# Four graph layers on one core: source tiles cut at multiples of 128 blocks, their addresses computed from one word

## What is computed

```python
x = _layernorm(x + L0(x, edge_attr))        # mean of edge_attr by src, three matmuls with ReLU and batch norm
x = _layernorm(x + L1(x))                   # relu((mean over edges of x[src], by dst, + x) @ W.T + b)
x = _layernorm(x + L2(x, edge_type))        # messages by type, mean by dst, a matmul, layer norm, GELU
x = _layernorm(x + L3(x, edge_weight))      # see below

def _L3_gnn_ref(node_features, edge_index, edge_weight, W, b, gamma, beta):
    ...
    norm = dinv[row] * w * dinv[col]
    x = node_features @ W
    msg = x[row] * norm[:, None]
    out = jax.ops.segment_sum(msg, col, num_segments=N) + b
    ...
```

## Time and profile before

| | us |
|---|---|
| median of three runs | 3749.47 (3747.87 to 3751.64) |
| the profiled execution | 3743.15 |
| its span | 3741.4 |
| mean granted clock of PE | 0.964 |

### The profile page before, as it was taken

One profiled execution on the slowest core, in us unless ns is written; L12 is line 12 of the kernel. 1 busy time (PEld: TensorE's weight loads), 2 busy tenths in 40 slices (PEclk: granted clock), 3 DMA queues, 4 the chain that ended last, 5 costly groups with the idle time before them and its releaser, 6 DMA issues.

```text
span 3741.4 us, 94994 instructions
## 1 busy us (share of the span) xinstructions
PE 2820.6 (75%) x23282; PEld 2453.3 (66%) x23283; DVE 2495.4 (67%) x7099; ACT 1517.8 (41%) x4312; POOL 1847.8 (49%) x2243
## 2 busy tenths in 40 slices
PE   8555544444439986887799689999999958887996
PEld 6232322222229975777799479999899957776995
DVE  7666666666647778555577777777666777554667
ACT  0111100000004445555577543222365348886765
POOL 4777777777763341777433354444521007774000
PEclk9999999999999997999899899999999989998998
DMA  6444444444448943778698035555378807885883
GB/s 216 150 150 141 149 143 146 147 143 149 141 131 285 292 144 104 279 274 280 216 293 274 9 115 175 177 179 183 126 241 248 263 30 273 272 283 194 289 286 123
DMA packets 419041, 721.75 MB, mean 193 GB/s; under 512 B 68624, under 2 KB 198169, under 8 KB 417932
## 3 DMA queue, kind: packets, MB, share of 16 engines
q1 hardware_dynamic: 330492, 494.35, 42.7%
q0 software_dynamic: 88464, 226.43, 16.1%
HBM read 481.26 MB, written 285.09 MB: 205 GB/s over the span
## 4 chain that ended last, share of the span: by engine, by line
PE 42%; POOL 23%; issue 13%; DMA 11%; DVE 5%; ACT 3%; SPq 2%; DVEq 2%; POOLq 1%; ACTq 0%
PE ps L1375 20%; POOL slots L750 19%; PE ps L1408 9%; DMA gbuf<-ring_raw,to_blk 8%; PE ps L1410 5%; POOL gbuf L804 3%; DMA ring_raw<-gbuf 2%; PE ps L1420 2%; PE ps L1250 2%; PE ps L1461 1%; DVEq L501 1%; PE ps L1452 1%; DVE stats L1935 1%; SPq L501 1%; ACT ring_raw L976 1%
## 5 line engine op out<-in xcount | busy, mean ns | idle before, releaser
L804 POOL DMA_INDIRECT gbuf<-ring_raw,to_blk x774 | 754.4, 975 | 727.4 <-DVE ring_raw L1868 257.9
L750 POOL DMA_INDIRECT slots<-ring_raw,idx_edges x782 | 751.4, 961 | 242.2 <-issue 242.2
L1375 PE MATMUL ps<-ring_raw,memory 128*128 128x128 f32 (+2 forms) x6576 | 784.6, 279 | 82.6 <-DVE memory L1836 49.2
L1375 PEld LDWEIGHTS ps<-ring_raw,memory 128*128 128x128 f32 x6576 | 764.5, 193 | 104.9 <-issue 56.3
L1836 DVE TENSOR_TENSOR memory<-dst_lane,lane_ids 128x512 f32<-128x512 f32 x774 | 535.1, 692 | 74.8 <-POOL dst_lane L768 51.7
L1286 PE MATMUL ps<-memory 128*49 128x343 bf16 (+6 forms) x784 | 263.5, 489 | 387.9 <-DVE memory L1732 386.6
L1408 PE MATMUL ps<-memory 128*128 x2752 | 497.8, 273 | 9.9 <-DVE memory L1877 7.5
L1846 DVE TENSOR_TENSOR memory<-memory,ps 128x128 f32 (+2 forms) x1032 | 294.6, 285 | 308.3 <-PE ps L1375 294.8
L935 ACT ACTIVATE memory<-lane_ids,dst_lane 128x128 f32<-128x128 f32 x1032 | 330.3, 392 | 403.2 <-PE ps L1375 246.1
L1410 PE MATMUL ps<-memory 128*128 x2752 | 477.4, 220 | 0.0
L1286 PEld LDWEIGHTS ps<-memory 128*49 128x49 bf16 x784 | 113.9, 159 | 530.4 <-DVE memory L1732 301.6
(11 more groups left out here) (283 smaller groups left out, 4781.6 us busy)
## 6 DMA issues: line engine op xcount, KB each, us to landing
ring_raw<-gbuf SPq DMA_DIRECT2D x669, 268.0 KB, 3.6
ring_raw<-in_edge_attr SPq DMA_DIRECT2D x111, 448.0 KB, 3.8
ring_raw<-slots SPq DMA_DIRECT2D x153, 272.0 KB, 4.1
zr<-lane_rows SPq DMA_DIRECT2D x87, 384.0 KB
zt<-lane_rows SPq DMA_DIRECT2D x87, 384.0 KB
memory<-lane_rows SPq DMA_DIRECT2D x84, 384.0 KB, 4.8
memory<-slots SPq DMA_DIRECT2D x105, 272.0 KB, 4.1
memory<-gbuf SPq DMA_DIRECT2D x105, 268.0 KB, 3.8
```

The source lines that it names most:

```text
L750: pool.indirect_dma_start(edges, bass.IndirectOffsetOnAxis(idx_edges[0:n, u, j:j + 1], 0), edge_rows[0:n, u, j, :], None).then_inc(scatter ...
L804: pool.indirect_dma_start(gbuf, bass.IndirectOffsetOnAxis(to_blk[:, t:t + 1], 0), node_rows[:, r, :], None, bounds_check=NBLK - 1, oob_is_ ...
L1375: ins = pe.matmul(bank(r % 3, width), hots[:, r, j * P:(j + 1) * P], rows[:, j, 0:width], start=j == 0, stop=j == BLK - 1)
```

## The change

The source tiles of the gathers are cut elsewhere. Blocks of the sorted list are taken 128 at a time from the list's start, whatever group they belong to: SPANS = 210 spans, 35 rounds (SR) of six. Where a group ends within a span, two groups share it. A pair of group and span is a step, and there are at most 210 + 49 - 1 = 258 of them, the same number as tiles before.

- `gather(1)` and `gather(3)`: PE still takes 258 steps, but a step adds to its span's bank, so a span with two groups gets two steps of matmuls and is copied and sent once. Four banks are used in turn. Ahead of its four matmuls a step does a matmul of one column with zeros (`new_bank`), which opens the next span's bank. ACT and POOL take 210 spans. `gather(2)` and its 258 sends are as before, over the new steps.
- PE takes one 16-bit word a round from `step_words`. It says which of the six steps begin a new span; from it PE computes for each step the bank, the next bank, the nodes' column and the count of `staged` to wait for. ACT takes three such words a round from `span_words`, for the counts of `gathered` it waits for.
- `reduce(0)` goes over the same 258 steps. Its payload now has nine words (`P_TYPED`, lane and type in one), and ACT keeps it by span, at a place it loads from a table (`at_pay`), and the target block of each step apart (`to_of`).
- DVE makes the new tables after the old ones (`span_tables`). POOL has two more operations on the payload at the start and fewer between `reduce(0)` and `gather(1)`.

```diff
+SPANS = -(-MAXB // P)
+SR = SPANS // RING
+BANKS = 4
...
-    return RR * (layer - 1)
+    return (0, SR, SR + RR, SR + RR + SR)[layer - 1]
...
-PAY = 8
-P_ONE, P_TYPE, P_W, P_DST, P_SRC, P_TO = 0, 1, 4, 5, 6, 7
+PAY = 9
+LIST = PAY - 1
+P_ONE, P_TYPE, P_W, P_DST, P_SRC, P_TYPED, P_TO = 0, 1, 4, 5, 6, 7, 8
...
+            steps.link(pool.tensor_scalar(pay8[:, :, P_TYPED], type_i, float(P), -float(P), ALU.mult, ALU.add))
+            pool.wait_ge(pays_ready, 7)
+            pool.tensor_tensor(pay8[:, :, P_TYPED], pay8[:, :, P_TYPED], pay8[:, :, P_SRC], ALU.add).then_inc(pays_ready, 1)
...
+                to = to_blk if layer == 2 else to_span
...
-                for i in range(RR):
+                for i in range(RR if layer == 2 else SR):
                     for r in range(RING):
                         scatter_block(i, r)
...
-            def keep_pays(h, odd):
+            def keep_pays(h, odd, at):
                 i = h * 2 + odd
                 for r in range(RING):
                     rows = rows_of(0, r, odd).rearrange("p (k w) -> p k w", k=BLK)
                     wait_rows(act, 0, h, r, odd)
-                    act.copy(pays[:, bass.ds(i * RING + r, 1), :].rearrange("p a (k w) -> p (a k) w", k=BLK),
+                    act.copy(to_of[:, bass.ds(i * RING + r, 1)], rows[:, 0, D + P_TO:D + P_TO + 1])
+                    act.wait_ge(pays_kept, i * RING + (RING + r))
+                    act.copy(pays_raw[:, bass.ds(at[r], BLK * PAY)].rearrange("p (k w) -> p k w", k=BLK),
                              rows[:, :, D:ROW_A]).then_inc(pays_kept, 1)
...
+                def send_round(i):
+                    words = nc.values_load_multi_w_load_instructions(
+                        span_words[:, bass.ds(i * (RING // 2), RING // 2)], engines=[ACT_E], min_val=0, max_val=65535,
+                        skip_runtime_bounds_check_because="words of 16 bits")[1]
                     for r in range(RING):
                         at = i * RING + r
-                        act.wait_ge(gathered, i * RING + (RING + base + r + 1))
+                        if r % 2 == 0:
+                            count = (words[r // 2] & 511) + (RING + GATHERED[layer])
+                        else:
+                            count = count + (words[r // 2] >> 9)
+                        act.wait_ge(gathered, count)
...
-                def gather_tiles(i):
-                    at = loaded(at_x, None, i, PE, (GROUPS - 1) * D)
+                def new_bank(to):
+                    pe.matmul(ps_flat[:, to], ident_h[:, :], none_h, start=True, stop=True, skip_group_check=True)
...
+                def gather_steps(i):
+                    word = nc.values_load_multi_w_load_instructions(
+                        step_words[:, bass.ds(i, 1)], engines=[PE], min_val=0, max_val=D * SPANS - 1,
+                        skip_runtime_bounds_check_because="the table holds such words")[1][0]
+                    first = (word >> 7) + STAGED[layer]
+                    span = word & 0x7F80
                     for r in range(RING):
+                        if r:
+                            span = span + (word & (2 << r)) * (D >> (r + 1))
+                        to = in_bounds((span * 4) & (BANKS - 1) * 512, (BANKS - 1) * 512)
+                        upon = in_bounds((span * 4 + 512) & (BANKS - 1) * 512, (BANKS - 1) * 512)
+                        node = in_bounds(i * (RING * D) + r * D - span, (GROUPS - 1) * D)
+                        if r == 3:
+                            first = first + (word & 3)
+                        pe.wait_ge(staged, first + (r % 3 + RING + 2 - BANKS))
+                        new_bank(bass.ds(upon, 1))
                         pe.wait_ge(src_hots, i * RING + (base + r + 1))
-                        pe.wait_ge(staged, i * RING + (base + r + 1))
                         for j in range(BLK):
-                            ins = pe.matmul(bank(r)[:, j * P:(j + 1) * P], hots[:, r, j * P:(j + 1) * P],
-                                            nodes[:, bass.ds(at[r], D)], start=True, stop=True)
+                            ins = pe.matmul(ps_flat[:, bass.ds(to + j * D, D)], hots[:, r, j * P:(j + 1) * P],
+                                            nodes[:, bass.ds(node, D)], start=False, stop=j == BLK - 1,
+                                            skip_group_check=True)
                         ins.then_inc(gathered, 1)
```

## The result

The kernel before ran in 3750.55 us (median of 4 runs, 3747.87 to 3754.14), the changed one in 3929.98 us (median of 4, 3928.31 to 3933.58): a ratio of 1.0486, 95% interval 1.0472 to 1.0500. The change makes this kernel 4.9% slower. Forecast were 3910 us and a range of 3825 to 4000.

What follows compares the result with a forecast made beforehand. POOL's sends, 1.28 us each, were taken to bound the gathers, and PE's sequencer after the change. 3743.15 us + 156 (gathers) + 5 (elsewhere) = 3904, with 6.3 for the median of runs 3910; range 3825 to 4000.

Steps and rivals of the forecast that it cites:

- POOL bounds before, PE's sequencer after: Gathers 1 and 3: POOL's sends at 1.28 us bound now; after the change PE's register instructions, about 0.10 us each, do.
- The round: Six steps of PE in gathers 1 and 3: 7.9 us of steps, 0.6 head, 1.2 load, together 9.7 us.
- The step: PE in gathers 1 and 3: 12 register instructions at 0.10 us plus five matmuls at 0.02, 1.30 us.
- The load: PE's register load each round of gathers 1 and 3, one word in place of six: taken as 1.2 us.
- The tail: POOL's work behind the last matmul of gathers 1 and 3 shrinks to the last send, giving back 9 us a stage.
- `gather(1)` +81: Layer 1 gather: 417 us of rounds, less 327.1 now and 9 of tail, makes it 81 us longer.
- `gather(3)` +75: Layer 3 gather: 417 us of rounds, less 333.5 now and 9 of tail, makes it 75 us longer.
- Elsewhere +5: `reduce(0)` +3 us for ACT's added copies and load, `span_tables` +2 us on DVE, POOL's added passes nothing.
- ACT and four banks "no cost": Gathers 1 and 3: a bank is asked for again 8 us later, ACT needs one to two: no cost.
- Rival 1: Gathers 1 and 3: register work hides behind queued matmuls, the array bounds, 288 us a stage, 3652 us total; chance 0.13.
- Rival 3: Gathers 1 and 3: array at the lower 1.2 GHz clock throughout, 533 us a stage, 4143 us total; chance 0.04.
- Queued matmuls behind a control instruction: PE: the skill's queuing rule would support hiding; the prediction held that rows 5 contradict it for matmuls with register-computed addresses.

Runs made afterwards that it cites:

- the loads of one word: Kernel before, with one 32-bit word loaded a round in place of six, used for all six tiles: 3752.22 us in one run.
- the smallest dose: Kernel before, each matmul's PSUM address computed in registers to the same value, 6 sequencer instructions a step (3 before) in five of six steps: 3750.13 us, ratio 1.0006.
- the doses: Kernel before, PSUM addresses computed in registers to unchanged values, with 6, 10 or 12 sequencer instructions in five of six steps: 3750.13, 3807.4 and 3905.0 us.
- the kernel with 16-bit tables: Changed kernel with bank, next bank, node and span loaded from a table, 24 words of 16 bits a round, instead of computed: 4390.34 us, ratio 1.1714.
- the fastest table kernel: Changed kernel with six banks, tables of 20 32-bit words, one wait for three steps, two rounds a loop turn: 3701.95 us, ratio 0.9875 to the kernel before.

## Why the prediction was right, point by point

**POOL bounds before, PE's sequencer after: right.** That POOL bounds before is shown by the loads of one word and by the smallest dose, which both leave the stages as they were. That the register work alone is enough for the loss is shown by the doses, and that it is the cause in the changed kernel itself by what less of it gives: 0.24 us a step for two instructions less, and 3702 us with all of the change but the arithmetic, the four banks and some waits, which were not taken away one by one from the changed kernel.

**The round: 9.7 us forecast, 9.76 measured, by two errors that cancel.** That is the mean from load to load in `gather(1)` (409.8 us for 42 rounds, by the row of loads below); 43 times the sum counts one head more than the stage has between its first and last matmul. The step was 1.48 us, not 1.30. Five of its instructions were mis-sized. Two of them, which compute the next bank and the node's address in four operations each, take 0.17 us from start to start where I had 0.10 for all: the price of a register instruction was taken from a few short ones. Three that stand ahead of a matmul take 0.13, not 0.12. Together 2 x 0.07 + 3 x 0.01 = 0.17. The sequencer's rows of the step from 1700.84 on (min/median/max ns, first and last start) show the long ones by the largest durations, 112 and 113 ns where the earlier trace rows had at most 46:

```profile
L1477 PEldq FUSED_REGOPS  x2: 42/77/112, 1701.1 to 1701.3; - x2
```

```profile
L1500 PEldq FUSED_REGOPS  x5: 42/51/113, 1701.5 to 1702.2; - x5
```

The load was the other error: 0.29 us in the median of `gather(1)` and 0.32 of `gather(3)`, where I had taken 1.2 between 0.89 and 1.75.

```profile
L1483 PEldq TENSOR_LOAD <-at_blk x43: 285/288/549, 1474.3 to 1884.1; - x43
```

```profile
L1483 PEldq TENSOR_LOAD <-at_blk x43: 283/317/545, 3172.1 to 3593.2; - x43
```

I had bounded a load of one word by loads of six and twelve, and scaled only by the DMA share. So 6 x 1.48 + 0.54 of head + 0.29 = 9.71. Against the forecast the steps are 1.0 us a round too small and the load 0.9 too large: that the sum fits is luck, and a range made from 0.09 to 0.107 us an instruction did not hold the 0.17 of a long one. The upper end of the range was also added up wrong: 0.107 and 1.75 give a round of 10.8 us and about 4010 in all, not 10.9 and 4022. The branch took its 0.2 us as before (208 ns, 207 in the earlier trace rows).

**The tail: right.** 9.3 and 8.9 us given back, 9 forecast.

**`gather(1)` +81 forecast, +81.8 measured; `gather(3)` +75 forecast, +87.5 measured.** The missing 12.5 us are layer 3's. Its instruction for the node's address has one operation more and lasts 131 ns instead of 113 (the row below), which adds 0.02 us to each step. Its fourth step has one more register instruction, 0.1. The load is 0.05 longer in the mean. That is 0.12 + 0.1 + 0.05 = 0.27 a round, x 43 = 11.6 us. The prediction used one round for both layers without looking at layer 3's own instructions.

```profile
L1500 PEldq FUSED_REGOPS  x1: 131/131/131, 3302.1 to 3302.1; - x1
```

**Elsewhere +5 forecast, +8.1 up to the end of `reduce(0)`.** ACT's copies did go in pairs 0.33 us apart (0.4 forecast). In the changed kernel and seven of its kin the start of `reduce(0)` lies at 1112.8 to 1115.8 us and the stage lasts 256.1 to 259.9, against 1110.0 to 1111.2 and 251.1 to 252.7 in the kernel before and four of its kin: 4 and 6 us in the mean, so this part was too small by half, for both together. The other 8.2 us of the table lie in stretches that the change doesn't touch. Half of them is the dense stage behind `reduce(1)`, 118.9 us before and 122.8 after; the dose of 6, with the code of before in that stage, has 121.3, and those of 10 and 12 have 122.6. So I take it as scatter between executions; the one of before that was profiled was a short one, 7 us under its median.

**ACT and four banks "no cost": right at this pace only.** In `gather(1)` of the changed kernel the instruction that waits for a bank starts 0.10 us behind the one before it in the mean of each step but the first, and 0.15 there, so there is next to no such wait. With less register work the four banks, with ACT's computed bank beside them, cost 61 us in one kernel and 189 in another.

**Rival 1 (the register work hides)** is out for this change, and its deciding point was put rightly where the sequencer passes the other bounds. Its time for full hiding, 3652, is 50 us under the 3702 of the kernel that comes closest. Of these `gather(1)` has 8 (296 us from first to last matmul against 288, a step being 1.00 us and not 0.95) and `gather(3)` 31 (319 us, with its waits for banks and longer gaps behind the loads); the rest is the smaller tail and the time elsewhere. **Rival 3 (the lower clock all through)** is out: the granted clock in the gathers was 0.99 and 0.98. It did show up where I hadn't looked for it, behind PE's 6 us stops in the kernel with 16-bit tables.

**Queued matmuls behind a control instruction.** Matmuls that were already queued did go on while a control instruction ran: in the timeline of the kernel with 16-bit tables, weight loads start until 1608.90 + 0.97 us, 1.5 us into a load of registers that began at 1608.4. To that extent the trace agrees with the Trainium skill's "Advanced Engine Details and Errata", Sequencer Loop. But only about twelve weight loads were queued at that point, and a matmul whose address was still to be computed was not among them: in the changed kernel the array stands idle 0.43 to 0.45 us in each of the steps shown above.

## What to carry to other kernels

Count the instructions of an engine's sequencer per step as a resource of its own, with the number of operations in each, and compare that sum with the array's time and with the slowest partner's: below the largest of them register work is free, above it each instruction counts in full, 0.1 to 0.17 us here. A change that takes work off the bounding engine by giving another one arithmetic should put the arithmetic into a table made once, and load it in 32 bits. When one bound is lifted, look again at the buffers that were ample before: four PSUM banks cost nothing at 2.0 us a span, and, with 0.2 us more of ACT's own between its wait and its copy, 61 and 189 us in kernels that could have run at 1.8 and 1.6.

## What the runs showed of the hardware that I had not expected

**Loads into registers.** The loads of 16-bit words went by the piece: one 0.29 us, three on ACT 0.90 in the median (0.30 each), 24 on PE 7.4 (0.31 each). Those of 32-bit words did not: in `gather(1)` one took 0.41 in the median, six 1.6 to 1.7, 20 took 1.8 and 24 took 2.2. Twelve in layer 2 took 0.9, so that the place counts more than the number. The DMA share was 0.77 in the one and 0.50 in the other, but it alone doesn't explain it: ACT's twelve in `reduce(0)` of the changed kernel took 0.78, at a share of 0.89. It stays open.

**Fused register instructions.** The long ones of the changed kernel (112 to 131 ns, 0.17 to 0.19 us from start to start) are not long by the number of their operations alone. In the fastest table kernel, one with the same four kinds of operation (multiply, add, multiply, add; so the program has it, the trace doesn't name them) is among these, of which none lasts over 65 ns:

```profile
L1495 PEldq FUSED_REGOPS  x975: 46/46/65, 1480.1 to 1759.9; - x195
```

What in them makes the difference was not tried and stays open. Who counts a sequencer's work has to take the price from an instruction of the same form, or measure it.

**The clock column in a stage with short matmuls.** In the scatter stage the profiled execution of the changed kernel shows a granted clock of 0.50, that of the kernel before 1.00, and that alone brings its mean down to 0.832; the three other executions of the changed kernel, of 3928 to 3934 us, have 0.970 to 0.972. The time isn't touched by it: the matmuls of the same 1000 us are busy for the same 450.8 and 450.6 us, and the kernel without the one-column matmul, at 1.00 there, starts `reduce(0)` at 1114.5, the changed one at 1115.0. First the changed kernel, then the kernel before:

```profile
100.00:1100.00 1000.00, 450.77 (x3007) 276.87 (x3007) 655.40 (x2655) 95.65 (x324) 757.44 (x785) 0.50 0.48 143
```

```profile
100.00:1100.00 1000.00, 450.58 (x3008) 277.34 (x3006) 650.48 (x2636) 95.16 (x324) 756.43 (x787) 1.00 0.44 142
```
